# Splitting the projection's weights at the end of the mixing stage, and its first product ahead of the last two tiles' turn

## The reference, cut to what matters

```
x_norm = layer_norm(x, norm_g, norm_b)
out1 = gat_conv(x_norm, src, dst, W1, ..., H1=4 heads of 192)
out2 = gat_conv(out1, src, dst, W2, ..., H2=2 heads of 96)
graph = concatenate([x, out2]) @ Wu + bu          # Wu: (768 + 192, 768)
x = x + graph + mix(xn)                           # mix: softmax-free attention, then @ Wo + bo
x = x + experts(layernorm(x))                     # top 2 of 8, gate = xt @ Wg + bg
```

## Time and profile before

| | |
|---|---|
| median of 3 runs | 963.11 us (962.73 to 963.61) |
| the profiled execution | 964.2 us, span of its core 962.4 us |
| mixing stage's last products end | 470.9 us |
| layer 1 on TensorE | 471.5 to 602.4 us |
| layer 2's units on TensorE | 641.2 to 694.3 us |
| first and second product of the projection | 698.9 and 701.3 us |
| experts | from 764 us |

### The profile page before, as it was taken

How to read it: one execution, slowest core, us unless ns; L and a number is a source line. 1 busy time by engine, 2 the same in 40 slices (tenths; PEclk the granted TensorE clock), 3 DMA queues, 4 the chain that set the end, 5 groups by cost and what they waited for, 6 DMA issues and landing times.

```text
span 962.4 us, 17237 instructions
## 1 busy us (share of the span) xinstructions
PE 912.5 (95%) x6379; PEld 670.4 (70%) x6381; DVE 746.1 (78%) x1704; ACT 350.1 (36%) x464; POOL 134.2 (14%) x153
## 2 busy tenths in 40 slices
PE   6899999989999999999999999989997899999995
PEld 5667676756665555567799999679866666666662
DVE  7878999997877799895889997889989544444443
ACT  5751212122235314314345552465446223232320
POOL 3400000000002000000000000020010344545441
PEclk9999999999999999999999999999998899999998
DMA  9610212246367689697792000189475668778860
GB/s 324 193 60 24 77 62 70 72 172 236 116 215 226 215 270 267 186 285 259 246 390 83 12 1 1 34 196 330 167 283 216 258 162 196 185 183 195 201 156 3
DMA packets 78844, 164.29 MB, mean 171 GB/s; under 512 B 28308, under 2 KB 47638, under 8 KB 75818
## 3 DMA queue, kind: packets, MB, share of 16 engines
q1 hardware_dynamic: 63402, 117.18, 35.9%
q0 software_dynamic: 10944, 38.22, 16.5%
q10 hardware_dynamic: 4416, 7.78, 2.2%
HBM read 109.13 MB, written 50.51 MB: 166 GB/s over the span
## 4 chain that ended last, share of the span: by engine, by line
PE 72%; DVE 18%; DMA 3%; issue 3%; ACT 2%; SPq 1%; DVEq 1%; ACTq 0%; POOLq 0%; POOL 0%
PE PS L2050 46%; PE PS L2323 15%; PE PS L2151 3%; DVE arena L1784 3%; PE PS L2521 2%; DVE arena L1611 1%; DVE arena L1432 1%; DVE arena L1617 1%; DMA arena<-in_L_ffn_W_dram 1%; PE PS L2162 1%; PE PS L2536 1%; PE PS L2342 1%; DVE arena L1594 1%; DVE arena L1497 1%; PE PS L2219 1%
## 5 line engine op out<-in xcount | busy, mean ns | idle before, releaser
L2050 PE MATMUL PS<-arena 128*128 128x384 f16 (+7 forms) x3396 | 561.5, 321 | 7.8 <-DVE arena L2040 3.0
L2050 PEld LDWEIGHTS PS<-arena 128*128 128x128 f16 (+2 forms) x3396 | 319.9, 99 | 214.3 <-issue 10.0
L2323 PE MATMUL PS<-arena 128*128 128x193 f32 (+1 forms) x1200 | 178.4, 310 | 3.2 <-DVE arena L1617 2.5
L2323 PEld LDWEIGHTS PS<-arena 128*128 128x128 f32 x1200 | 176.4, 191 | 5.3 <-DVE arena L1617 3.8
L1189 ACT ACTIVATE arena<-arena,AS 128x1250 f32<-128x1250 f32 x60 | 79.9, 1338 | 74.7 <-DVE arena L1611 74.6
L1617 DVE SCALAR_TENSOR_TENSOR arena<-arena 128x1250 f32<-128x1250 f32 x60 | 87.1, 1453 | 5.8 <-PE PS L2323 5.7
L1497 DVE TENSOR_SCALAR arena<-arena 128x240 f16<-128x240 f16 x324 | 88.8, 274 | 0.0
L1611 DVE SCALAR_TENSOR_TENSOR arena<-arena,AS 128x1250 f32<-128x1250 f32 x55 | 83.0, 1508 | 0.0
L1496 DVE TENSOR_SCALAR arena<-arena 128x128 f16<-128x128 f16 x324 | 79.8, 246 | 0.1
L2039 DVE SCALAR_TENSOR_TENSOR arena<-PS,arena 128x768 f32<-128x768 f32 x27 | 25.8, 957 | 62.6 <-PE PS L2050 62.6
L1321 ACT ACTIVATE arena<-PS 128x1536 f16<-128x1536 f16 x27 | 39.1, 1449 | 74.8 <-PE PS L2521 74.8
(11 more groups left out here) (276 smaller groups left out, 914.0 us busy)
## 6 DMA issues: line engine op xcount, KB each, us to landing
arena<-in_L_ffn_W_dram SPq DMA_DIRECT2D x48, 384.0 KB, 3.8
fr_d<-arena SPq DMA_DIRECT2D x48, 384.0 KB, 3.3
arena<-fr_d SPq DMA_DIRECT2D x16, 1152.0 KB, 12.3
arena<-in_x_dram SPq DMA_DIRECT2D x18, 384.0 KB, 5.6
arena<-rr_d SPq DMA_DIRECT2D x4, 1280.0 KB, 8.6
g_d<-arena SPq DMA_DIRECT2D x10, 388.0 KB, 2.4
acc_d<-arena SPq DMA_DIRECT2D x10, 384.0 KB, 3.4
xf_d<-arena ACTq DMA_DIRECT2D x10, 384.0 KB, 3.5
```

Of the source, the lines that this page charges most:

```text
L2050: m = T.matmul(out, left[i][x], right[i][y], start=first and i + r == 0, stop=last and 3 * i + r == n - 1)
L2323: m = T.matmul(ps[sum_bank(h, b)][:, r * (C + 1):(r + 1) * (C + 1)], (PT1 if deep == 3 else PT)[i % deep][:, d * P:(d + 1) * P], feats, st ...
```

## The change

Three things are moved; no value of the output changes.

1. **The weights' split** leaves layer 2. ScalarE now takes the high part of block 0 into a spare place (`wuh0`) right behind its last `zq_high` of the mixing stage, waits for VectorE's low part of block 0, takes the high part of block 1, waits for its low part, and then copies `wuh0` to its final place. VectorE takes the two low parts at tile 8 of the last chunk, so behind its last `zq_low` and ahead of the set-up of `h2x` and of layer 1's first `slopes`. Each low part waits for its high part, and block 1's high part waits for block 0's low part, since the parts now overwrite the 32-bit weights in place. All of it stays where `WUB` was.
2. **fin(0)** goes ahead of the last turn (`out_turned(5)`). It waits for the first three of the last head's five pairs (banks 6 and 7 are free then) and for `out_low(3)`, which VectorE now does inside `head_result`, behind tile 7. `fin(1)` waits for the whole head. The filling products between the last turn and `fin(0)`, and between `fin(0)` and `fin(1)`, are gone.
3. **The first two sums** (tiles 0 and 1) are added in two halves of 384 columns each, with a signal of TensorE for each half.

```diff
@@ -219,9 +219,10 @@
         mask2 = reg(6 * UNIT, NT * NP // 2).bitcast(BF16).rearrange("p (a b) -> p a b", a=NT)
         assert 6 * UNIT + NT * NP // 2 <= 9 * UNIT <= O_G
         out2T = reg(12 * UNIT, H2 * NP, KS + 1).bitcast(F16).rearrange("p (r h n) -> p r h n", r=2, h=H2)
-        wuh = reg(12 * UNIT + H2 * NP, D, KS + 1).bitcast(F16).rearrange("p (h n) -> p h n", h=H2)
-        wul = (reg(12 * UNIT + H2 * NP + D, HALF, KS + 1).bitcast(F16), reg(O_W2, HALF, KS + 1).bitcast(F16))
-        assert 12 * UNIT + H2 * NP + D + HALF <= min(14 * UNIT, O_RR + 2 * NP)
+        wul = (reg(O_W2, HALF, KS + 1).bitcast(F16), reg(O_W2 + D, HALF, KS + 1).bitcast(F16))
+        wuh = (reg(O_W2 + D + HALF, HALF, KS + 1).bitcast(F16), reg(O_W2 + HALF, HALF, KS + 1).bitcast(F16))
+        wuh0 = reg(O_OH + 3072 + 640, HALF, KS + 1).bitcast(F16)
+        assert 12 * UNIT + H2 * NP <= min(14 * UNIT, O_RR + 2 * NP) and O_OH + 3072 + 640 + HALF <= O_G
         OUT2 = [(h, a, min(a + 512, NP)) for h in range(H2) for a in range(0, NP, 512)]
         NOUT = len(OUT2) // H2
 
@@ -861,7 +862,7 @@
             sp.dma_start(bgrow, bg.partition_broadcast(P)).then_inc(s_small_in, 16)
             for u in freed:
                 experts(u)
-            sp.wait_ge(s_fin_psum, NT)
+            sp.wait_ge(s_fin_psum, 2 * NT)
             sp.wait_ge(s_rown_ready, NT - 2)
             for u in late:
                 experts(u)
@@ -1179,6 +1180,14 @@
                         for j in range(KC):
                             zq_high(n * KC + j)
 
+            act.wait_ge(s_w2_in, 16 * 5)
+            act.wait_ge(s_q_ready, NJ)
+            a.activation(wuh0[0:KS + 1, :], WUB[0:KS + 1, 0, :], ACT.Copy, scale=UP).then_inc(s_projection_ready, 1)
+            act.wait_ge(s_projection_ready, 2)
+            a.activation(wuh[1][0:KS, :], WUB[0:KS, 1, :], ACT.Copy, scale=UP).then_inc(s_projection_ready, 1)
+            act.wait_ge(s_projection_ready, 4)
+            a.activation(wuh[0][0:KS + 1, :], wuh0[0:KS + 1, :], ACT.Copy).then_inc(s_projection_ready, 1)
+
             def expo(unit, h, t):
                 i = unit - U0
                 if i in RELU:
@@ -1208,11 +1217,6 @@
                 h, a0, a1 = OUT2[n]
                 act.wait_ge(s_o2t_psum, 4 + n + 1)
                 a.activation(out2T[0:KS, 0, h, a0:a1], PS[0:KS, 2 * 512 + a0:2 * 512 + a1], ACT.Identity, bias=b2c[:, h:h + 1]).then_inc(s_o2t_ready, 1)
-
-            def projection_high(h):
-                r = KS + 1 - h
-                act.wait_ge(s_w2_in, 16 * 5)
-                a.activation(wuh[0:r, h, :], WUB[0:r, h, :], ACT.Copy, scale=UP).then_inc(s_projection_ready, 1)
 
             def layer1():
                 for i in range(H1 * NT):
@@ -1261,8 +1265,6 @@
                         row_out(2 + i // 2)
                     if h and t + 1 in SCALED:
                         head_scaled(H1, SCALED[t + 1])
-                    if h and t in (4, 5):
-                        projection_high(t - 4)
                     if h and t in (7, 8, 9):
                         out_high(t - 7)
 
@@ -1686,6 +1688,12 @@
                     if t > t0:
                         for c in conv_of_t[t]:
                             conv_low(c)
+                    if t == NT - 2:
+                        for h in range(H2):
+                            dve.wait_ge(s_projection_ready, 1 + 2 * h)
+                            r = KS + 1 - h
+                            hi = (wuh0, wuh[1])[h]
+                            V.scalar_tensor_tensor(wul[h][0:r, :], WUB[0:r, h, :], UP, hi[0:r, :], ALU.mult, ALU.subtract).then_inc(s_projection_ready, 1)
                     if t in IND_T:
                         edge_or_not(IND_T[t])
                     ns = list(MAX_T.get(t, ()))
@@ -1736,7 +1744,7 @@
                     i = V.tensor_tensor(h2, h2, scaled[part].rearrange("p t (h c) -> p t h c", h=H2), ALU.add)
                 i.then_inc(s_col_ready, 1)
 
-            def head_result(n):
+            def head_result(n, lows=()):
                 h, C = (n, CW) if n < H1 else (n - H1, C2)
                 dve.wait_ge(s_head_out, 5 * n)
                 for d in range(NT):
@@ -1752,6 +1760,9 @@
                         k = V.tensor_scalar(h2x[:, d, h, 0:C2], v, rden[:, b, r:r + 1], None, ALU.mult)
                     if r:
                         k.then_inc(s_head_out, 1)
+                    if d == 7:
+                        for m in lows:
+                            out_low(m)
 
             def layer1():
                 for i in range(H1 * NT):
@@ -1819,18 +1830,13 @@
                         denominators(H1 + h - 1)
                 for n in range(NOUT):
                     out_low(n)
-                dve.wait_ge(s_projection_ready, 4)
-                for h in range(H2):
-                    r = KS + 1 - h
-                    V.scalar_tensor_tensor(wul[h][0:r, :], WUB[0:r, h, :], UP, wuh[0:r, h, :], ALU.mult, ALU.subtract).then_inc(s_projection_ready, 1)
-                    dve.wait_ge(s_projection_ready, 5 + h)
-                head_result(H1 + H2 - 1)
+                head_result(H1 + H2 - 1, (NOUT,))
                 dve.wait_ge(s_head_out, 5 * (H1 + H2))
 
             layer1()
             layer2()
 
-            for n in range(NOUT, 2 * NOUT):
+            for n in range(NOUT + 1, 2 * NOUT):
                 out_low(n)
 
             seq8 = seq[:, 0:NE].rearrange("p (a e) -> p a e", a=1)
@@ -1903,9 +1909,16 @@
                 if s < NT:
                     g = [s < b for _, b in X1G].index(True)
                     dve.wait_ge(xs_in[g], 16 * ((NT + XS - 1 - g) // XS + 1))
-                    dve.wait_ge(s_fin_psum, s + 1)
+                    b = (6, 0)[s % 2] * 512
+                    if s < 2:
+                        for c in range(2):
+                            dve.wait_ge(s_fin_psum, 2 * s + c + 1)
+                            half = X[:, s, c * HALF:(c + 1) * HALF]
+                            i = V.scalar_tensor_tensor(half, ps[b // 512 + c][:, 0:HALF], 1 / UP, half, ALU.mult, ALU.add)
+                        i.then_inc(s_x2_ready, 1)
+                if 2 <= s < NT:
+                    dve.wait_ge(s_fin_psum, 2 * s + 2)
                     x2 = X[:, s, :].rearrange("p (a n) -> p a n", a=2)
-                    b = (6, 0)[s % 2] * 512
                     V.scalar_tensor_tensor(x2, PS[:, b:b + 1024].rearrange("p (a n) -> p a n", a=2)[:, :, 0:HALF], 1 / UP, x2, ALU.mult, ALU.add).then_inc(s_x2_ready, 1)
                 t = s - 1
                 if 0 <= t < NT:
@@ -2422,16 +2435,11 @@
                     row(3)
                 if h and t in (4, 5, 6):
                     out_turned(t - 4)
-            for n in range(NOUT):
-                pe.wait_ge(s_o2l_ready, n + 1)
-                keep_warm(4 if n else 16, 2 + n)
-                out_turned(NOUT + n)
-            pe.wait_ge(s_head_out, 5 * (H1 + H2))
-            keep_warm(4, 6)
-
             def fin(t):
                 if t == 0:
-                    pe.wait_ge(s_projection_ready, 6)
+                    pe.wait_ge(s_projection_ready, 7)
+                    pe.wait_ge(s_head_out, 5 * (H1 + H2) - 2)
+                if t == 1:
                     pe.wait_ge(s_head_out, 5 * (H1 + H2))
                 if t >= 2:
                     pe.wait_ge(s_x2_ready, t - 1)
@@ -2441,8 +2449,15 @@
                     for h in range(H2):
                         r = KS + 1 - h
                         m = product(ps[(6, 0)[t % 2] + c][:, 0:HALF], [(out2T[0:r, 0, h, t * P:(t + 1) * P], out2T[0:r, 1, h, t * P:(t + 1) * P])],
-                                    [(wuh[0:r, h, cs], wul[h][0:r, cs])], first=h == 0, last=h == H2 - 1)
-                m.then_inc(s_fin_psum, 1)
+                                    [(wuh[h][0:r, cs], wul[h][0:r, cs])], first=h == 0, last=h == H2 - 1)
+                    m.then_inc(s_fin_psum, 1)
+
+            for n in range(NOUT):
+                pe.wait_ge(s_o2l_ready, n + 1)
+                keep_warm(4 if n else 16, 2 + n)
+                if n == NOUT - 1:
+                    fin(0)
+                out_turned(NOUT + n)
 
             def transposes(t):
                 pe.wait_ge(s_rown_ready, t + 1)
@@ -2475,9 +2490,9 @@
                 return T.matmul(ps[RANK_BANK[q]][:, 0:(b - a) * NE], upper, OSh[:, a:b, :].rearrange("p t e -> p (t e)"), start=first, stop=last, skip_group_check=True)
 
             for s in range(NT + 5):
-                if s < NT:
+                if 0 < s < NT:
                     fin(s)
-                if s < NT + 3:
+                if 0 < s < NT + 3:
                     keep_warm(4, 5)
                 if 0 <= s - 4 < NT - 1:
                     transposes(s - 4)
```

## The result

The changed kernel took 966.91 us (median of 20 runs, 962.15 to 971.86), the kernel before 963.15 us on the same chips (20 runs, 960.77 to 966.82). The ratio is 1.0033, 95% interval 1.0022 to 1.0045: slower, by 2.1 to 4.3 us (0.0022 and 0.0045 of 963.15). The profiled execution took 968.05 us, 965.2 of it span; before it was 964.2 and 962.4.

A forecast was written before the change was run, and what follows sets the result against it. TensorE, busy 95% of the span and never waiting in layer 1, was taken as the bound. The split with its clock fall (3.3 us) plus the tail (0.1) gave 3.4 us on the median 963.11: 966.5 us, range 964.4 to 968.3.

The forecast's parts named there:

- the gate's bias: In the tail: its load lands at 705.9 to 706.1, VectorE waits for it, a loss of 0.1 us.
- the tail's term: Reordered tail: VectorE reaches the gate's weights 1.3 us earlier but waits for the bias, net loss 0.1 us.
- The split's price: Mixing stage's end: VectorE loses 3.2 us; layer 1's units 0, 1, 2 start 1.7, 2.1, 2.8 us late; 2.8 stays.
- The clock: Layer 1's start: TensorE's wait drops its clock to 1.2 GHz for 3.4 us, raising the term from 2.8 to 3.3.
- rival (a): Layer 1's start: TensorE's clock stays up, so 2.8 + 0.1 us, 966.0; chance 0.24.
- its sign: End of layer 1: TensorE 2.8 to 3.3 us late would show the forecast right.
- From there nothing gives time back: Layer 1 after unit 2: TensorE is never idle, so the 2.8 us delay stays to the end.
- The tail's order: Tail: `fin(0)` starts at 697.95, 0.9 us earlier; VectorE waits before `out_low(3)` and `out_low(5)`, reaches gate's weights at 704.35.
- issuing behind them by 701 changes little: Tail: the bias, queued behind the loads of `X`, lands where it did though issued at 700.8, not 698.93.
- Rival (b): Tail: the bias's load moves with its later issue, so 3.3 + 1.9 us, 968.3; chance 0.14.
- (d): The mixing stage costs 2.8 us but the bias is early: 2.8 - 1.6 = 1.2 us, 964.3; chance 0.10.
- Layer 2: ScalarE loses two instructions of 0.83 us, but VectorE sets the pace there, so 0.

The follow-up runs named there:

- `c5`: The changed kernel with the first mask loaded by plain copies instead of transposing ones; 966.83 us against 963.15 for the kernel before, ratio 1.0026.
- `e_hidden`: The changed kernel with plain mask copies and the weights' split moved on to the end of layer 1; 964.20 us, ratio to before 1.0018.
- `b5`: The kernel before with only the first mask's transposing copies replaced by plain copies; ratio to before 1.0007.
- `b6`: The same code as `b5`, the kernel before with plain mask copies, run again; ratio to before 1.0005.
- `e_mix`: The kernel before with plain mask copies and only the split moved to the mixing stage's end, old tail; 967.20 us against 962.69, ratio 1.0036.

## Why the prediction was right

The forecast was 3.4 us; the ratio gives 3.2, the medians 3.8. It was right as a whole, but not by its own sum: one step failed (the gate's bias, with the sign of the tail's term), and two terms that the sum did not have made up for it: the time outside the span, and in the profiled execution of after a later wait in layer 1. That they cancelled is luck.

**The split's price: right.** VectorE lost 464.22 - 461.10 = 3.1 us between its last `zq_low` and the end of the second low part (forecast 3.2). Counted from the mixing stage's last product, unit 0 came 1.7 us later (forecast 1.7), unit 1 2.2 (2.1), SP's load 3.2 (3.2), GpSimd's ones 3.2, and unit 2 2.6 (2.8; 0.05 us lay between the end of the ones and unit 2, not 0.26).

**The clock: right, and not in every execution.** Two of the three profiled kernels with this front had the fall, where the forecast put it, and lost 3.37 and 3.38 us by the end of layer 1, against 3.3. From the rows this adds up: 1.70 us of wait before unit 0 and half of the 3.3 us at 1.2 GHz, 3.35 together, with the waits before units 1 and 2 under the slow stretch. The profiled execution of after had no fall (rival (a)), and should have lost 2.8 by the forecast.

**What stood in its place: a wait the forecast did not look for.** After lost 3.88 without a fall, more than the 2.8 to 3.3 that the forecast named as its sign. The load of tiles 5 to 9 goes out behind the first, and took 9.6 us there; in the other seven traces it took 7.6 to 8.4. Before, it took 7.8, the ones were written by 486.7 and unit 5 started at 487.9, so 1.2 us was in hand. A load that is issued 3.2 us later for units that start 2.6 us later has 0.6 us less, and a transfer that takes 1.8 us more uses up the rest and 1.2 us beyond it, the 1.24 of unit 5. With the 7.6 to 8.4 us of the other traces there would have been no wait to speak of (an estimate from these rows), so this one belongs to one slow transfer in one execution; the change took half of what was in hand. "From there nothing gives time back" was right; that nothing more would be taken was assumed.

**The tail's order: right.** Put into the times of before (less 3.48, by which the last unit and the filling products came later), `fin(0)` started at 698.1 (forecast 697.95), the last turn at 700.0 (699.9), `out_low(5)` ended at 701.45 (701.25), and VectorE reached the gate's weights at 704.5 (704.35). The gaps before `out_low(3)` and `out_low(5)` are there.

**The gate's bias: the step that failed.** The forecast had it land at 705.9 to 706.1 and put a loss of 0.1 us on the tail. It landed at 708.44, so at 704.96 in the times of before; VectorE waited 0.50 us for it in place of the forecast's 1.6, and the tail gained 0.94. The error is in "issuing behind them by 701 changes little": the bias did not only keep its place, it moved forward by 0.9 us. The gain is no chance of one trace: the new tail took 10.89, 10.97 and 11.06 us (after, `c5`, `e_hidden`), the old one 11.83, 12.15 and 11.92 (before, `b5`, `b6`). Rival (b) had it the other way round, and (d) was right in sign, with 0.9 in place of 1.6.

**Time outside the span: missing.** The sum carried the 1.8 us outside the span over unchanged; it became 2.5 in most runs. What it is stays open. So 3.4 to 3.9 at the front, less 0.9 in the tail, and 0.7 outside: 3.2 to 3.7, where the forecast had 3.3 + 0.1.

**Layer 2:** nothing, as forecast (+0.06). VectorE's idle 5.7 us at the end of layer 1, which the trace of before has as well, played no part in the forecast; in the trace of `e_hidden` the split fits there for nothing.

## What to carry to other kernels

Work freed on a tuned path is worth only what the next thing that is late lets through; and work moved to a stage's seam pays for its hand-overs between engines too (here 1.2 us of waiting on 1.9 of work). Look for the place where the receiving engine already waits longer than the moved work with its hand-overs takes: by the traces the same five instructions cost 3.4 us at one seam and nothing at the other, though the time of `e_hidden` isn't told from before's. When a load is delayed, go through every later load on the same queue against its own slack, not only the first that is waited for.

## What the runs showed of the hardware

A small load's time from issue to landing says little about the load. SP issues the rows of `X` first and the gate's bias behind them. Issued 7.5 to 7.9 us after the first of `X` the bias took 6.97 us (before), 7.27 (`b5`), 7.05 (`b6`) and 7.50 (`e_mix`); issued 9.9 us after it took 4.03 (after), 4.11 (`c5`) and 4.19 (`e_hidden`). Counted from the issue of `X` it landed after 14.9 to 15.2 us in the first four and after 13.9 to 14.1 in the other three: in none did it land before the last of `X` (issued at 691.9 and 12.5 us under way before, so until 704.4, and until 708.0 after), and asking 2 us later brought it 1 us earlier. The first half agrees with what the Trainium skill says in "DMA: Bandwidth & Descriptors", section "Queues, rings and completion order", that on each DMA engine the descriptors are taken in the order of the ring; that asking later can bring it earlier is this case's own row, and its cause was not tested. One difference is in the traces. From 1.5 to 0.5 us before the bias landed, the DMA engines moved 0.41 MB before, all but 2 of 46 packets being 8 KB or larger, and 0.10 MB after, with 109 of 122 packets under 512 B. So before, large packets were beside the last of the small ones, and after they were not.

The same wait of 2.3 us on TensorE was followed by a fall of the clock in two profiled executions and by none in a third. Half of 3.3 us is 1.65 us of work lost, but `c5` was through layer 1 only 0.8 us later than after would have been with no late load (3.37 against 1.70 + 0.47 + 0.43 = 2.60, an estimate from the rows of after), since the slow stretch lay over waits that come without it.
